# Quantised feed-forward of a two-layer transformer block on one core: the clip and the scaling of activations on ScalarE and GpSimd, and a software pipeline over half tiles

## What is computed

```python
def _mx_linear(x, w):
    return jnp.einsum('bsh,oh->bso', _q_act(x), _q_w(w))   # activations clipped at 7.5, weights at 6.0
gate = _mx_linear(x, w_gate)          # 512 -> 2048
up = _mx_linear(x, w_up)              # 512 -> 2048
inter = jax.nn.silu(gate) * up
return _mx_linear(inter, w_down)      # 2048 -> 512
```

## Time and profile before

| what | value |
|---|---|
| three runs, median (lowest to highest) | 1871.81 us (1865.91 to 1873.47) |
| the profiled execution | 1870.53 us, its span from first to last instruction 1868.7 us |
| mean granted clock of PE in it | 0.894 of full speed |

### The profile page before, as it was taken

The page is one execution under the profiler, slowest core; times in us unless marked ns, Lnnn a source line. Parts: engine busy times, 40 slices in busy tenths (PEclk is TensorE's granted clock), DMA queues, the critical chain, the costliest instruction groups (busy, mean ns, idle before and its releaser), DMA issues. The chain is left out here.

```text
span 1868.7 us, 31243 instructions
## 1 busy us (share of the span) xinstructions
PE 1484.8 (79%) x10376; PEld 777.9 (42%) x10395; DVE 1112.7 (60%) x1785; ACT 980.8 (52%) x1503; POOL 635.6 (34%) x557
## 2 busy tenths in 40 slices
PE   6666666677776775999999711899999999999994
PEld 2444455543333332444444310444444444444442
DVE  3999999788888896888886472205415140541000
ACT  4999999733232233777777440344444444444442
POOL 3000000010000000788888535435445444544432
PEclk9778777788898897999999765999999999999998
DMA  9311100000000000000000256315335151531113
GB/s 336 135 46 46 46 1 1 29 1 1 0 0 0 0 0 1 3 2 3 2 3 3 88 190 249 117 35 163 111 86 168 26 165 34 163 95 34 30 28 102
DMA packets 49246, 118.69 MB, mean 64 GB/s; under 512 B 5536, under 2 KB 5792, under 8 KB 48576
## 3 DMA queue, kind: packets, MB, share of 16 engines
q1 hardware_dynamic: 34832, 88.53, 14.0%
q0 software_dynamic: 8176, 18.65, 5.1%
q10 hardware_dynamic: 6144, 10.28, 1.8%
HBM read 84.21 MB, written 37.43 MB: 65 GB/s over the span
## 5 line engine op out<-in xcount | busy, mean ns | idle before, releaser
L1622 PE MATMUL PS<-R 128*128 (+1 forms) x1872 | 432.7, 381 | 8.3 <-issue 7.2
L1776 DVE TENSOR_SCALAR R<-wring 128x1024 f16<-128x1024 f32 x56 | 61.5, 1108 | 382.6 <-PE PS L1645 349.2
L425 ACT ACTIVATE R<-R 128x512 bf16<-128x512 f32 x448 | 278.9, 715 | 9.4 <-PE PS L445 3.9
L1622 PEld LDWEIGHTS PS<-R 128*128 128x128 f16 x1872 | 179.5, 98 | 217.6 <-issue 19.7
L445 PE MATMUL PS<-R,ident_b 128*128 128x256 bf16 (+1 forms) x1056 | 168.6, 321 | 83.1 <-ACT R L425 79.1
L1645 PE MATMUL PS<-R 128*128 (+1 forms) x936 | 214.8, 379 | 1.2 <-ACT R L1732 1.2
L1812 POOL TENSOR_TENSOR R<-R 128x512 f32<-128x512 f32 x78 | 113.3, 1453 | 292.0 <-ACT R L1720 181.0
L871 PE MATMUL PS<-R 128*128 128x512 bf16 x495 | 141.9, 436 | 78.6 <-DVE R L807 60.4
L1036 DVE TENSOR_REDUCE R<-PS 128x1 f32<-128x512 f32 x256 | 166.6, 686 | 45.2 <-PE PS L1218 42.6
L1014 POOL TENSOR_TENSOR R<-R 128x512 f32<-128x512 f32 x128 | 166.6, 1302 | 27.8 <-ACT R L1141 12.2
L1141 ACT ACTIVATE R<-PS 128x512 f32<-128x512 f32 x256 | 144.4, 598 | 41.3 <-PE PS L1232 40.8
(11 more groups left out here) (262 smaller groups left out, 2522.3 us busy)
## 6 DMA issues: line engine op xcount, KB each, us to landing
wring<-in_L_ffn_w_kernel_dram SPq DMA_DIRECT2D x48, 512.0 KB, 5.3
slot_rows<-R SPq DMA_DIRECT2D x1, 10023.0 KB, 40.3
R<-slot_rows ACTq DMA_DIRECT2D x39, 257.0 KB, 2.7
R<-in_L_ffn_w_kernel_dram SPq DMA_DIRECT2D x16, 512.0 KB, 5.6
wring<-in_L_ffn_wo_kernel_dram SPq DMA_DIRECT2D x16, 512.0 KB, 4.5
R<-in_L_ffn_wo_kernel_dram SPq DMA_DIRECT2D x16, 512.0 KB, 4.7
X<-in_x_dram SPq DMA_DIRECT2D x4, 1024.0 KB, 9.0
R<-in_L_ffn_w_up_dram SPq DMA_DIRECT2D x4, 1024.0 KB, 10.3
```

The lines of the kernel that those rows point to most:

```text
L425: nc.scalar.activation(marks[:, j * S:(j + 1) * S], SIM[:, tile * S:(tile + 1) * S], ACT.Sign, bias=cfloat[:, tile:tile + 1], scale=-1.0). ...
L1622: mm = nc.tensor.matmul(bank[2 * half + g], ZT[n][:, (4 * pz + k) * P:(4 * pz + k + 1) * P], weights(place, at), start=(i % 12 == 0), stop ...
```

## The change

- `quantize_act` is split over three engines. DVE keeps the block maxima, the scale, the reciprocal and the cut to fp8 (`scales`, then the cut in `z_scale` or `inter_scale`). The mask and the factor take their second operand from SBUF tables (`bexp`, `b16`), as `tensor_tensor` and `scalar_tensor_tensor` where they were `tensor_scalar`. Before the cut a semaphore wait stands in place of a drain.
- The clip is done by ACT with two Relus (`z_cap`, `inter_cap`): u = relu(cap - q), then c = relu(2 cap - u), which is the clipped value plus cap.
- GpSimd takes off cap and multiplies by the scale, in pieces of 512 columns (`pool_b`).
- The order is written out over half tiles u: DVE works on u, ACT caps u - 1 and copies u - 2, PE makes gate and up of u + 1, turns u - 2 and multiplies down u - 3. The buffers `bin_`, the cut, the capped and final values, `bit2` and the turn bank (4 and 7) are doubled, the scales fourfold. The loops are gone, all 16 tiles are written out. Each `down` of a half counts `down_ps`; the residual of tile i comes after the products of half 2i + 5.
- Four small memsets for the tables and the two caps stand ahead of those in `pool_selectors`, and ACT and DVE wait for them at the stage's start.

The diff, cut to its core:

```diff
-        def quantize_act(v, src, n, dst, base, done):
...
-            nc.vector.tensor_scalar(bq[:, 0:n], bf8[:, 0:n], 7.5 / 64, -7.5 / 64, ALU.min, ALU.max).then_inc(q_step, 1)
-            v.wait_ge(q_step, base + 6)
-            nc.vector.tensor_tensor(blocks(dst), blocks(bq[:, 0:n]), spread(sc, nb), ALU.mult).then_inc(done, 1)
+        def scales(v, src, am, pw, sc, ri, n, step, base):
+            nc.vector.tensor_reduce(am, blocks(src), AX, ALU.max, apply_absolute_value=True).then_inc(step, 1)
+            v.wait_ge(step, base + 1)
+            nc.vector.tensor_tensor(pw.bitcast(I32), am.bitcast(I32), bexp[:, 0:n], ALU.bitwise_and).then_inc(step, 1)
+            v.wait_ge(step, base + 2)
+            nc.vector.scalar_tensor_tensor(out=sc, in0=pw, scalar=TINY, in1=b16[:, 0:n], op0=ALU.max,
+                                           op1=ALU.mult).then_inc(step, 1)
+            v.wait_ge(step, base + 3)
+            nc.vector.reciprocal(ri, sc).then_inc(step, 1)
+            v.wait_ge(step, base + 4)
...
+            def inter_scale(u):
+                v.wait_ge(inter_ready, 2 * u + 2)
+                if u > 3:
+                    v.wait_ge(ib_ready, 2 * u - 6)
+                scales(v, bin_[u % 2], bam, bpw, bsc[u % 4], bri, 1024 // BLK, i_step, u * 4)
+                if u > 1:
+                    v.wait_ge(i_under, u - 1)
+                nc.vector.tensor_tensor(blocks(biq[u % 2]), blocks(bin_[u % 2]), spread(bri, 1024 // BLK), ALU.mult,
+                                        saturate=False).then_inc(i_cut, 1)
...
+            for u in range(2 * NT):
+                for n in range(2):
+                    product(u, n)
+                if u % 2 and u > 4:
+                    residual((u - 5) // 2)
+                inter_scale(u)
+                if u % 2 == 0 and u // 2 + 2 < NT:
+                    z_scale(u // 2 + 2)
+                if u % 2 and u > 4:
+                    moments((u - 5) // 2)
...
+            def inter_final(u):
+                pool.wait_ge(i_capped, u + 1)
+                pool.wait_ge(i_cut, u + 1)
+                if u > 1:
+                    pool.wait_ge(it_ps, u - 1)
+                for n in range(2):
+                    c = slice(512 * n, 512 * n + 512)
+                    nc.gpsimd.tensor_scalar(bic[u % 2][:, c], bic[u % 2][:, c], -CAP, None, ALU.add).then_inc(i_signed, 1)
+                    pool.wait_ge(i_signed, 2 * u + n + 1)
+                    nc.gpsimd.tensor_tensor(blocks(bib[u % 2][:, c]), blocks(bic[u % 2][:, c]),
+                                            spread(bsc[u % 4][:, 16 * n:16 * n + 16], 16), ALU.mult).then_inc(ib_ready, 1)
...
+            for u in range(2 * NT):
+                inter_final(u)
+                if u % 2 == 0 and u // 2 + 2 < NT:
+                    z_final(u // 2 + 2)
...
+            for u in range(2 * NT + 3):
+                if u + 1 < 2 * NT:
+                    gate_up(u + 1, 0)
+                    gate_up(u + 1, 1)
+                if u % 2 == 0 and u // 2 + 1 < NT:
+                    zturn(u // 2 + 1)
+                if u == 2 * NT + 1:
+                    pe_projection(pe)
+                if 0 <= u - 2 < 2 * NT:
+                    turn(u - 2)
+                if 0 <= u - 3 < 2 * NT:
+                    down(u - 3)
...
+            def inter_cap(u):
+                act.wait_ge(i_cut, u + 1)
+                if u:
+                    act.wait_ge(i_capped, u)
+                nc.scalar.activation(biu, biq[u % 2], ACT.Relu, bias=bcap, scale=-1.0).then_inc(i_under, 1)
+                act.wait_ge(i_under, u + 1)
+                if u > 1:
+                    act.wait_ge(ib_ready, 2 * u - 2)
+                nc.scalar.activation(bic[u % 2], biu, ACT.Relu, bias=bcap2, scale=-1.0).then_inc(i_capped, 1)
...
             act.wait_ge(ln_ready, 2)
+            act.wait_ge(const_b, 4)
             norm(0)
+            z_cap(0)
             norm(1)
...
+            zcopy(0)
+            z_cap(1)
+            norm(2)
+            for n in range(2):
+                silu(0, n)
+            for u in range(2 * NT + 2):
+                if 0 <= u - 1 < 2 * NT:
+                    inter_cap(u - 1)
+                if u == 2 * NT:
+                    act_projection(act)
+                if u + 1 < 2 * NT:
+                    silu(u + 1, 0)
+                if u % 2 and u // 2 + 2 < NT:
+                    z_cap(u // 2 + 2)
+                    if u // 2 + 3 < NT:
+                        norm(u // 2 + 3)
+                if u + 1 < 2 * NT:
+                    silu(u + 1, 1)
+                if 0 <= u - 2 < 2 * NT:
+                    icopy(u - 2)
+                if u % 2 == 0 and u // 2 + 1 < NT:
+                    zcopy(u // 2 + 1)
...
             pool_b_weights(pool)
             pool_ln(pool, 1)
+            pool_b(pool)
             pool_ln(pool, 2)
```

More of the change, by code:

```diff
@@ L837, in dve_b @@
[L837 to L846, removed]
-            dve_ln_var(v, 2, 0)
-            chain(NT - 1, 1, (NT - 1) * 18 + 12)
-            finish(NT - 1)
+            v.wait_ge(const_b, 4)
@@ L889, in down @@
                 for c in range(8):
-                    k = half * 8 + c
-                    mm = nc.tensor.matmul(bank[5], bit2[:, c * P:(c + 1) * P], WDT[:, k * D:(k + 1) * D],
+                    k = u % 2 * 8 + c
+                    mm = nc.tensor.matmul(bank[5], bit2[u % 2][:, c * P:(c + 1) * P], WDT[:, k * D:(k + 1) * D],
                                           start=(k == 0), stop=(k == 15))
[L893 to L905, removed]
+                mm.then_inc(down_ps, 1)
@@ L924, in act_b @@
-        def act_b(act):
[L925 to L928, removed]
-                                     scale=rstd[:, bass.ds(i, 1)]).then_inc(z_ready, 1)
-            def zcopy(i, b):
-                act.wait_ge(zt_ps, i + 1)
-                if beyond(i, 1):
-                    act.wait_ge(gu_ps, 8 * i - 8)
-                nc.scalar.copy(bzt[b], bank[6].bitcast(BF16)[:, 0:512]).then_inc(zt_sb, 1)
-            def silu(i, half):
-                h = 2 * i + half
-                for n in range(2):
-                    act.wait_ge(gu_ps, 4 * h + 2 * n + 1)
-                    if beyond(h, 0):
-                        act.wait_ge(inter_ready, 2 * h + n - 1)
-                    nc.scalar.activation(bsg[:, n * 512:(n + 1) * 512], bank[n], ACT.Silu).then_inc(silu_sb, 1)
-            def icopy(i, half):
-                h = 2 * i + half
-                act.wait_ge(it_ps, h + 1)
-                if half:
-                    act.wait_ge(down_half, i + 1)
-                elif beyond(i, 0):
-                    act.wait_ge(down_ps, i)
-                nc.scalar.copy(bit2, bank[4].bitcast(BF16)).then_inc(it_sb, 1)
-            def body(i, b, last=False):
-                if not last:
-                    norm(i + 2)
-                silu(i, 1)
-                icopy(i, 0)
-                zcopy(i + 1, 1 - b)
-                silu(i + 1, 0)
-                icopy(i, 1)
@@ new lines, in act_b, with norm, z_cap, zcopy @@
+        def act_b(act):
+            def norm(j):
+                if j:
+                    act.wait_ge(z_cut, j)
+                nc.scalar.activation(bz, X[:, j * D:(j + 1) * D], ACT.Identity, bias=nmr[:, j:j + 1],
+                                     scale=rstd[:, j:j + 1]).then_inc(z_ready, 1)
+            def z_cap(j):
+                act.wait_ge(z_cut, j + 1)
+                if j:
+                    act.wait_ge(z_capped, j)
+                nc.scalar.activation(bzu, bzq, ACT.Relu, bias=bcap, scale=-1.0).then_inc(z_under, 1)
+                act.wait_ge(z_under, j + 1)
+                if j:
+                    act.wait_ge(zb_ready, j)
+                nc.scalar.activation(bzc, bzu, ACT.Relu, bias=bcap2, scale=-1.0).then_inc(z_capped, 1)
+            def zcopy(j):
+                act.wait_ge(zt_ps, j + 1)
+                if j > 1:
+                    act.wait_ge(gu_ps, 8 * j - 8)
+                nc.scalar.copy(bzt[j % 2], bank[6].bitcast(BF16)[:, 0:512]).then_inc(zt_sb, 1)
+            def silu(u, n):
+                act.wait_ge(gu_ps, 4 * u + 2 * n + 1)
+                if u:
+                    act.wait_ge(inter_ready, 2 * u + n - 1)
+                nc.scalar.activation(bsg[:, n * 512:(n + 1) * 512], bank[n], ACT.Silu).then_inc(silu_sb, 1)
+            def inter_cap(u):
+                act.wait_ge(i_cut, u + 1)
+                if u:
+                    act.wait_ge(i_capped, u)
+                nc.scalar.activation(biu, biq[u % 2], ACT.Relu, bias=bcap, scale=-1.0).then_inc(i_under, 1)
+                act.wait_ge(i_under, u + 1)
+                if u > 1:
+                    act.wait_ge(ib_ready, 2 * u - 2)
+                nc.scalar.activation(bic[u % 2], biu, ACT.Relu, bias=bcap2, scale=-1.0).then_inc(i_capped, 1)
+            def icopy(u):
+                act.wait_ge(it_ps, u + 1)
+                if u > 1:
+                    act.wait_ge(down_ps, u - 1)
```

(1 more changed line is left out.)

187 lines of the change are left out of this document (81 added, 106 removed).

## The result

The changed kernel takes 1802.65 us in the median (1801.05 to 1805.12, 4 runs), the kernel before 1872.28 (1865.91 to 1873.47, 4 runs). The ratio is 0.9636 with a 95% interval of 0.961 to 0.9661. The prediction was 1821 with a range of 1790 to 1858. The sign came out, and the gain is 69.6 us where 50 to 51 were forecast. Of the mechanism, DVE's chain and its waits behind POOL's multiplies came out. That POOL's own row of steps would fill the tile had not been forecast.

What follows compares the result with a forecast made beforehand. DVE's chain bounds the stage at 19.33 us a tile; 6.3 leave, 13.0 stay, and 2.7 of waiting behind GpSimd make p = 15.7. Time 1569.2 + 16p = 1820.4, say 1821 us, range 1790 to 1858.

Steps and rivals of the forecast that it cites:

- DVE's chain is the tile, 6.3 us leave it: Stage from first norm to last `nmr`: clip, final multiply and waits leave DVE, 19.33 us a tile becoming 13.0.
- ACT's lengths: ACT, a tile: four Relus over 1024 at 1.15, two z Relus at 0.7; 11.8 us in all, not the bound.
- POOL's subtraction: GpSimd's add of a constant per 512 elements: 0.77 us taken, bounds 0.6 and 0.95; five a tile.
- What they share: DVE steps with two SBUF inputs and GpSimd steps exclude each other: GpSimd holds 9.9 us a tile, DVE wants 4.2.
- the layout: One tile's steps laid out in time across the engines: period 15.3 to 16.1 us, taken 15.7, of which 2.7 waiting.
- The signs: Expected in the trace: tile 15.7 us, cuts up to 2.4, 32-wide steps up to 1.2, GpSimd about 65% busy.
- PE's clock: PE idles 2.0 us before each half, so the clock costs nothing; low level would add 3 us per gate-and-up pair.
- the formula: Stage end = 421.4 + 16p and time = 1569.2 + 16p, p being the tile's period in us.
- Beginning and end: Stage's edges: first product on ACT at 414.5, 3.4 us later; 15.6 us from the last cut to the end.
- The one in which sharing costs nothing: Rival: GpSimd and DVE do not delay each other in this stage; p = 13.0, 1777 us; chance 0.11.
- POOL at its upper bound: Rival: GpSimd's pair takes 0.95 + 1.45, 2.1 us a tile more; p = 17.7, 1852 us; chance 0.16.
- The slower one: Rival: GpSimd becomes the bound, deciding from a pair of 3.2 us; at 1.5 + 2.0, p = 20.5, 1897; chance 0.09.

Runs made afterwards that it cites:

- the order alone: Against the changed kernel, clip and final multiply go back to DVE, without Relus or POOL's steps; new order kept: 1866.85 us, ratio 0.9961.

## Why the prediction was right, and where not

- **DVE's chain is the tile, 6.3 us leave it.** Right for what leaves and what stays: 13.0 was forecast for its own work, 12.35 is left in the changed kernel's tile, and 12.2 in the others. The rest of the difference may be the register work of the loops and the drains, which I had left in; no run times it by itself. In the changed kernel DVE is no longer quite the tile: POOL's row of steps is, 0.3 us above it. The order alone is worth 8 us, so the offload carries the gain.
- **ACT's lengths.** Right: the Relus take 1.15 and 1.16 us (1024) and 0.72 (512), with one table load. ACT is not the bound. The rule of the Trainium skill ("ScalarE: Activation LUTs", rules for kernel authors) on where min and max belong would have put the loss on ACT; 104.5 of 138 us busy say that it was free enough.
- **POOL's subtraction.** Wrong, and the term that was mis-sized: 0.77 taken and 0.95 as the upper end, measured 1.49 to 1.54. The row it was taken from is of a step with two operations, which I read as the cost of any such step. The multiply was 1.05 to 1.12 for 1.2.
- **What they share.** Right for the multiply. For the subtraction right only in its first 0.62 us; the layout had it exclude DVE from end to end. The layout had 2.7 us of waiting a tile from both; 1.24 came in the tile above, all behind multiplies, because the cuts fell behind the part that excludes. The two errors, a subtraction too short and a waiting too long, pull in opposite ways. POOL's own 13.8 replaced DVE's 15.7, and the forecast of the tile was 1.9 us too long.
- **The signs.** Of those that were named, the tile (13.8 for 15.7), the cuts (1.23, once 1.96, for up to 2.4) and POOL's share (129.6 of 138 us, 94%, for 65%) did not come; the mask steps (up to 0.90, for up to 1.2) and PE's clock did. Cuts at 1.22 throughout had been named as a sign of being wrong, and came but for one. That the time still fell into the range is in part luck: a tile of 13.8 is its lower edge by the formula, and the ends of the stage, which took 8 us more than forecast, drew the time inwards.
- **Beginning and end.** The first product comes 12.7 us after the start of the first norm, 12.4 forecast. Behind the last cut there were 652.73 - 635.32 = 17.4 us, 15.6 forecast: POOL, still at the half before, starts the last one at 639.02, 1.2 after its Relus are done (637.78), and needs 5.4 us for it in place of 4.35. And the formula took 8.75 us of DVE work out of the outer tiles; the last cut came some 6 us later than by it, since with POOL as the limit they save little. With p = 13.8 it gives an end of 642.2, 644.7 with the stage's later start, measured 652.7: of 30 us that the tile was overestimated 8 came back here.
- **PE's clock.** Right for this kernel, 0.99 in the middle of the stage. That it can matter was seen with the order alone.
- **The rivals.** The one in which sharing costs nothing (1777 us) was close for the cuts, but the masks' 1.24 us of waits say that it costs something; the kernel that comes nearest to it is the one without multiplies, 12.6 us a tile and 1782 us. POOL at its upper bound happened in part: a pair of 2.6, more than its 2.4, and yet faster, because the price was reckoned as waits of DVE, and what the subtraction is longer by makes none. The slower one did not come near its point, a pair of 3.2.

## What to carry to other kernels

When work is moved to an engine that shares something with the one it is taken from, two sums bound the result, each engine's own steps and each engine's waits behind the other; lowering one may do nothing, or harm, as long as the other stands. Before the length of a step is taken from a row, look at its number of operations and at where its constants come from, not only at its shape. And order and offload are to be timed apart: here the order was 8 us of 70.

## What the runs showed of the hardware

- GpSimd's tensor-scalar over 512 elements takes 1.49 us with one operation and a constant in the instruction, in bf16 and float32, in place or apart, 0.62 with two operations and two constants in the instruction, and 0.77 with two operations and both constants from SBUF.
- The long form waits for a running DVE step with two SBUF inputs (1.49 becomes 2.34 and more), and holds such a step up only in its first 0.62 us: one that starts in the first 0.5 us waits until then, and a cut that starts after 0.6 us takes its usual 1.23. The short form (0.62) and the multiply (1.05) exclude it both ways over their whole length. The Trainium skill ("SBUF — State Buffer", who interferes with whom) has whichever comes second blocked for the whole instruction; the traces agree for the multiply and the short form, and not for the long one, where they decide.
- DVE's tensor-scalar over 32 elements waits behind GpSimd's multiply (0.57 us in the median, 0.19 undisturbed), and over 33 elements with differently shaped operands it does not (0.19). That fits the Trainium skill's condition for using both ports ("VectorE: DVE Perf Modes", mode 2×_2P): outermost dimensions both even, or equal.
